# A four-layer graph network on one core: part of the second pass's product computed inside the first pass, from column tiles still on chip

## The reference, cut to what matters

```
x1 = LN(x  + adj @ (scale * (adj @ (x @ w0))) + bias0)       # layer 0: two products with adj
x2 = LN(x1 + relu(inv_deg * (a*adj + (1-a)*I) @ x1 @ W.T + b))   # layer 1: row sums of adj give inv_deg
x3 = LN(x2 + layer2(x2))    # one product for z, then distances z z^T, 4 nearest, second product
x4 = LN(x3 + relu([x3, adj @ x3] @ W.T + b))                 # layer 3
```

## Time and profile before

| what | us |
|---|---|
| runs: median of 3 | 1589.72 |
| runs: lowest, highest | 1587.08, 2805.07 |
| profiled execution, its own time | 1597.85 |
| profiled execution, span first to last instruction | 1596.3 |
| PE busy, PEld busy in that span | 1446.2, 748.6 |
| DVE, ACT, POOL busy | 836.0, 465.3, 208.9 |

### The profile page before, as it was taken

One profiled execution on the slowest core, in us unless ns is written; L12 is line 12 of the kernel. 1 busy time (PEld: TensorE's weight loads), 2 busy tenths in 40 slices (PEclk: granted clock), 3 DMA queues, 4 the chain that ended last, 5 costly groups with the idle time before them and its releaser, 6 DMA issues.

```text
span 1596.3 us, 20924 instructions
## 1 busy us (share of the span) xinstructions
PE 1446.2 (91%) x7300; PEld 748.6 (47%) x7300; DVE 836.0 (52%) x1278; ACT 465.3 (29%) x979; POOL 208.9 (13%) x267
## 2 busy tenths in 40 slices
PE   6888888887999999999999888999999499878997
PEld 4555555554444444444444433444444144433554
DVE  6667667664222133323222379999998046543122
ACT  4656565653000000000000056666665000000010
POOL 1111111110000000000000000000000447763000
PEclk9999999999999999999999999999999799989999
DMA  9999998888899888888777500013333889889773
GB/s 312 332 334 340 340 323 314 311 323 332 340 343 345 335 314 312 316 324 331 304 283 283 184 7 1 14 54 120 123 124 115 283 321 371 310 321 361 284 284 130
DMA packets 127677, 418.98 MB, mean 262 GB/s; under 512 B 10657, under 2 KB 44033, under 8 KB 104577
## 3 DMA queue, kind: packets, MB, share of 16 engines
q1 hardware_dynamic: 78272, 331.37, 55.9%
q0 software_dynamic: 19088, 71.83, 11.8%
q10 hardware_dynamic: 30256, 15.00, 3.2%
HBM read 353.14 MB, written 65.01 MB: 262 GB/s over the span
## 4 chain that ended last, share of the span: by engine, by line
PE 56%; DVE 16%; DMA 10%; issue 7%; POOL 5%; ACT 5%; DVEq 0%; ACTq 0%; POOLq 0%; SPq 0%
PE acc L1010 12%; PE acc L1011 12%; PE acc L1012 12%; POOL gath_all L434 5%; DVE hT L865 5%; DVE wz_sb L866 5%; DMA at_scratch<-region 4%; PE pt L1054 3%; DMA gath_all<-y_scratch,wz_sb 2%; DVE region L818 2%; PE pt L1116 2%; PE pt L1119 2%; PE pt L1118 2%; PE pt L1117 2%; PE pt L1012 2%
## 5 line engine op out<-in xcount | busy, mean ns | idle before, releaser
L1010 PE MATMUL acc<-region,yop 128*128 128x512 f16 x850 | 326.8, 385 | 63.7 <-DVE region L818 39.1
L1011 PE MATMUL acc<-region,yop 128*128 128x512 f16 x850 | 326.2, 384 | 0.0
L1012 PE MATMUL acc<-region,yop 128*128 128x512 f16 x850 | 325.8, 383 | 0.0
L592 ACT ACTIVATE region<-pt 128x512 f32<-128x512 f32 x256 | 149.8, 597 | 114.8 <-PE pt L1119 79.6
L818 DVE SCALAR_TENSOR_TENSOR region<-pt,region 128x512 f16<-128x512 f32 x200 | 128.9, 685 | 94.2 <-ACT region L499 93.5
L1054 PE MATMUL pt<-ident,region 128*128 128x128 f32 x1024 | 153.7, 278 | 8.3 <-DMA region<-in_adj 8.3
L1010 PEld LDWEIGHTS acc<-region,yop 128*128 128x128 f16 x850 | 83.6, 98 | 156.1 <-DVE region L818 51.2
L1054 PEld LDWEIGHTS pt<-ident,region 128*128 128x128 f32 x1024 | 129.7, 144 | 55.2 <-issue 9.5
L865 DVE MAX8 hT<-region 128x8 f32<-128x4096 f32 x32 | 141.5, 4421 | 11.4 <-ACT region L592 10.6
L499 ACT ACTIVATE region<-pt 128x512 f16<-128x512 f32 x200 | 112.6, 593 | 106.9 <-PE pt L1054 64.1
L1012 PEld LDWEIGHTS acc<-region,yop 128*128 128x128 f16 x850 | 83.9, 99 | 102.9 <-issue 4.4
(11 more groups left out here) (221 smaller groups left out, 1904.7 us busy)
## 6 DMA issues: line engine op xcount, KB each, us to landing
region<-at_scratch SPq DMA_DIRECT2D x180, 1280.0 KB, 7.3
region<-in_adj SPq DMA_DIRECT2D x64, 1024.0 KB, 9.0
at_scratch<-region POOLq DMA_DIRECT2D x40, 768.0 KB, 7.1
region<-at_scratch SPq DMA_DIRECT2D x100, 256.0 KB, 3.7
at_scratch<-region POOLq DMA_DIRECT2D x40, 512.0 KB, 7.5
x_scratch<-xout ACTq DMA_DIRECT2D x24, 256.0 KB, 6.2
yop<-in_x SPq DMA_DIRECT2D x4, 512.0 KB, 10.8
xin<-in_x POOLq DMA_DIRECT2D x8, 256.0 KB, 3.5
```

The lines of the kernel that those rows point to most:

```text
L592: nc.scalar.activation(near[i % 2][:, j * CHUNK:(j + 1) * CHUNK], pt[n % NEAR_BANKS][:, :], ACT.Copy).then_inc(near_copied, 1)
L1010: nc.tensor.matmul(into, y[:, 0, kt, :], high, start=(kt == 0), stop=False)
L1011: nc.tensor.matmul(into, y[:, 0, kt, :], low, start=False, stop=False)
L1012: return nc.tensor.matmul(into, y[:, 1, kt, :], high, start=False, stop=(kt == KT - 1))
```

## The change

1. **Early products.** `early_tiles(c)` = max(0, 4(c-1)): 0, 0, 4, 8, 12, 16, 20, 24 for the eight chunks. In pass 0, while chunk c's tile kt is on chip, PE also multiplies it by pass 1's operand tile kt, if kt is below `early_tiles(c)` (those operand tiles come from chunks up to c-2 of pass 0 and exist already). The sum goes into PSUM bank `pxT`. At kt = 30 of such a chunk ACT copies it, scaled, into `xT` and stores it to a new DRAM tensor `part_scratch`. In pass 1, chunk c begins at tile `early_tiles(c)`; POOL loads the stored part into `xT`, and DVE (in place of ACT) makes `hT` as acc + part, for c = 2 to 7.
2. **Loads of pass 1.** Only tiles that pass 1 still multiplies are loaded (`UNITS1`), the first unit of a chunk in part. The first chunk's five units wait each for its own stretch of the on-chip memory (`early_slot`) in place of one wait for all of pass 0.
3. **Row sums in pieces.** Each unit is summed in four 128x512 pieces, two on DVE (even kt) and two on ACT (odd kt).
4. **Lag.** `LAG` = 4, and it runs over chunk ends: the first four tiles of chunk c+1 are transposed between the products of chunk c's last four. Within a tile, transposes and products now alternate: transpose 0, (early products), product, transpose 1, product, transpose 2, product, transpose 3.
5. **Places.** Pass 0's `hT` copy on ACT at kt = 7 (was 8), PE's projection at kt = 11 (was 8), DVE's epilogue at kt = 14 and 15 (was 16). In pass 1 the projection is placed four tiles after the chunk's first tile. PE's code for passes 0 and 1 is written out for all eight chunks; ACT's for pass 0 for four of them.

The core of the diff:

```diff
-LAG = 3
+LAG = 4
+ROW_PIECES = 2
+    part_dram = nc.dram_tensor("part_scratch", [NCH, P, CHUNK], F32).ap()
+        def early_tiles(c):
+            return max(0, (c - 1) * TPC)
+
+        UNITS1 = [(c, u, max(0, early_tiles(c) - KEPT - u * UNIT)) for c in range(NCH) for u in range(UPC)
+                  if KEPT + (u + 1) * UNIT > early_tiles(c)]
...
@@ SP, load_natural @@
-                        half = c * (NAT_UNITS // 2) + (u - 4) // 2 + 1
-                        sp.wait_ge(rows_summed_dve if u % 2 == 0 else rows_summed_act, half)
+                        sp.wait_ge(rows_summed_dve, before * ROW_PIECES)
+                        sp.nop(nofuse=True)
+                        sp.wait_ge(rows_summed_act, before * ROW_PIECES)
...
-            sp.wait_ge(tr_done, NCH * KT)
-            sp.wait_ge(rows_summed_dve, NCH * NAT_UNITS // 2)
-            sp.wait_ge(rows_summed_act, NCH * NAT_UNITS // 2)
-            sp.wait_ge(acc_full, NCH)
-            for s in range(2):
-                for part in range(len(STORES)):
-                    sp.wait_ge(stage_stored[s][part], 16 * NCH * UPC // 2)
+            def early_slot(u):
+                done = (NCH - 1) * NAT_UNITS + min(6 + u, NAT_UNITS)
+                sp.wait_ge(tr_done, done * TPC)
+                sp.wait_ge(rows_summed_dve, done * ROW_PIECES)
+                sp.wait_ge(rows_summed_act, done * ROW_PIECES)
+                if u == UPC - 2:
+                    sp.wait_ge(stage_used, NCH * (UPC - 1))
+                if u == UPC - 1:
+                    sp.wait_ge(acc_full, NCH)
+                for s in range(2):
+                    units = NCH * UPC // 2 if u >= UPC - 2 + s else (UPC + 1 - s) // 2
+                    for part in range(len(STORES)):
+                        sp.wait_ge(stage_stored[s][part], 16 * units)
+
+            for k, (c, u, k0) in enumerate(UNITS1):
+                if c == 0:
+                    early_slot(u)
+                else:
+                    before = max(b for b in range(k) if UNITS1[b][1] == u)
+                    if u == UPC - 1:
+                        sp.wait_ge(acc_full, nth(ALL, 1, UNITS1[before][0]))
+                    else:
+                        sp.wait_ge(unit_used, used1(before))
+                sp.dma_start(ring[u][:, k0:, :, :].rearrange("p k h n -> p (k h n)"),
+                             at_dram[c, u, :, k0 * 2 * CHUNK:]).then_inc(unit_loaded[u], 16)
...
@@ POOL, pass 1 @@
+            for c in range(NCH):
+                if c == 2:
+                    pool.wait_ge(part_stored, 16 * (NCH - 2))
+                if c > 2:
+                    pool.wait_ge(hT_ready, nth(ALL, 1, c - 1))
+                if c >= 2:
+                    pool.dma_start(xT[:, :], part_dram[c, :, :]).then_inc(part_loaded, 16)
+                load_xin(1, x_dram[0], c, c == 0)
...
@@ ACT, split_high @@
-                    if kt % 8 == 6:
+                    if kt % 2 == 1:
+                        u, t = divmod(kt, TPC)
...
+                        nc.scalar.activation(discard[:, 0:CHUNK], nat[u % 4][:, t, :], ACT.Copy,
+                                             accum_out=rs_part[par][:, u, t:t + 1]).then_inc(rows_summed_act, 1)
...
+                    if kt == KT - 2 and not (isinstance(c, int) and c < 2):
+                        act.wait_ge(part_full, c - 1)
+                        if not isinstance(c, int) or c > 2:
+                            act.wait_ge(part_stored, 16 * (c - 2))
+                        nc.scalar.activation(xT[:, :], pxT[:, :], ACT.Copy, scale=1.0 / (A_SCALE * Y_SCALE[0])
+                                             ).then_inc(part_ready, 1)
+                        act.wait_ge(part_ready, c - 1)
+                        act.dma_start(part_dram[bass.ds(c, 1), :, :].rearrange("c p n -> (c p) n"), xT[:, :]
+                                      ).then_inc(part_stored, 16)
...
@@ DVE, epilogue of pass 1 @@
+                if p == 1 and not (isinstance(c, int) and c < 2):
+                    dve.wait_ge(part_loaded, 16 * (c - 1))
+                    dve.wait_ge(acc_full, n)
+                    dve.wait_ge(nat_full, n - 1)
+                    nc.vector.scalar_tensor_tensor(hT[:, :], acc[par][:, :], 1.0 / (A_SCALE * Y_SCALE[0]), xT[:, :],
+                                                   ALU.mult, ALU.add).then_inc(hT_ready, 1)
...
@@ DVE, split_low @@
-                    if kt % 8 == 2:
...
+                    if kt % 2 == 0:
+                        u, t = divmod(kt, TPC)
+                        if t == 0:
+                            dve.wait_ge(nat_loaded[u % 4], 16 * (c * 2 + u // 4 + 1))
+                        nc.vector.tensor_reduce(rs_part[par][:, u, t:t + 1], nat[u % 4][:, t, :],
+                                                AXX, ALU.add).then_inc(rows_summed_dve, 1)
...
@@ PE, pass 0 @@
+            def products_of(c, par, kt, between):
+                hi, lo = stored(c, par, kt)
+                pe.wait_ge(low_done, c * KT + kt + 1)
+                if kt < early_tiles(c):
...
+                    nc.tensor.matmul(pxT[:, :], yh, hi, start=(kt == 0), stop=False)
+                    nc.tensor.matmul(pxT[:, :], yh, lo, start=False, stop=False)
+                    early = nc.tensor.matmul(pxT[:, :], yl, hi, start=False, stop=final)
...
+                nc.tensor.matmul(acc[par][:, :], yh, hi, start=(kt == 0), stop=False)
+                between(1)
+                nc.tensor.matmul(acc[par][:, :], yh, lo, start=False, stop=False)
+                between(2)
+                last = nc.tensor.matmul(acc[par][:, :], yl, hi, start=False, stop=(kt == KT - 1))
...
+                    turn(0)
+                    if kt >= LAG:
+                        products_of(c, par, kt - LAG, turn)
+                    elif not first(c):
+                        products_of(c - 1, 1 - par, KT + kt - LAG, turn)
+                    else:
+                        turn(1)
+                        turn(2)
+                    turn(3)
...
@@ PE, pass 1 @@
+                        if p == 1 and kt < early_tiles(c):
+                            continue
```

More of the change, by code:

```diff
@@ L249, in late_loads, with each_chunk @@
             return LATE_SLOTS[:k].count(slot)
-        def each_chunk(eng, body):
-            body(0, 0, 0)
-            body(1, 1, 0)
-            with eng.Fori(1, NCH // 2) as pair:
+        def each_chunk(eng, body, unrolled=2):
+            for c in range(unrolled):
+                body(c, c % 2, c // 2)
+            with eng.Fori(unrolled // 2, NCH // 2) as pair:
                 body(pair * 2, 0, pair)
@@ new lines, in split_high @@
+                    if kt == 7 and not first(c):
+                        act_epilogue(act, 0, c - 1, 1 - par)
+                    if kt == KT - 2 and not (isinstance(c, int) and c < 2):
[7 more added lines that the diff above has]
+                                      ).then_inc(part_stored, 16)
@@ L837, in _ @@
             each_chunk(dve, split_low)
-            counted(0, NCH - 1, lambda: epilogue(0, NCH - 1, 1))
+            scale_projected(NCH - 1)
+            counted(0, NCH - 1, lambda: split_projected(NCH - 1))
             close(0)
@@ L1006, in pe_epilogue, with products @@
                 pe_epilogue_at(pe, kt, p, c)
-        def products(p, into, kt, high, low):
+        def products(p, into, kt, high, low, first_tile=0):
             y = yop[OPERAND[p]]
-            nc.tensor.matmul(into, y[:, 0, kt, :], high, start=(kt == 0), stop=False)
+            nc.tensor.matmul(into, y[:, 0, kt, :], high, start=(kt == first_tile), stop=False)
             nc.tensor.matmul(into, y[:, 0, kt, :], low, start=False, stop=False)
@@ L1027, in setup_transposes, with stored @@
                 nc.tensor.transpose(setup_rows, hT[0:rows_j, 0:P], ident[0:rows_j, 0:rows_j]).then_inc(setup_pe, 1)
-            def transposing_chunk(c, par, m):
-                def products_of(kt):
-                    pe.wait_ge(low_done, c * KT + kt + 1)
-                    if kt < KEPT:
-                        hi, lo = (kept[:, bass.ds(c, 1), kt, h, :].rearrange("p c n -> p (c n)") for h in range(2))
-                    else:
-                        s = (par * UPC + (kt - KEPT) // UNIT) % 2
-                        hi, lo = (stage[s][:, (kt - KEPT) % UNIT, h, :] for h in range(2))
-                    if first(c) and kt % XT_PART == 0:
-                        pe.wait_ge(y0_ready, kt // XT_PART + 1)
-                    if kt == 0 and not (isinstance(c, int) and c < 2):
-                        pe.wait_ge(hT_ready, c - 1)
-                    last = products(0, acc[par][:, :], kt, hi, lo)
-                    if kt == KT - 1:
-                        last.then_inc(acc_full, 1)
-                    elif kt >= KEPT and (kt - KEPT) % UNIT == UNIT - 1:
-                        last.then_inc(stage_used, 1)
+            def stored(c, par, kt):
+                if kt < KEPT:
+                    return [kept[:, bass.ds(c, 1), kt, h, :].rearrange("p c n -> p (c n)") for h in range(2)]
```

(10 more changed lines are left out.)

116 lines of the change are left out of this document (68 added, 48 removed).

## The result

The changed kernel takes 1549.01 us, median of 4 runs (1545.57 to 1577.11), against 1592.13 for the kernel before; the ratio is 0.970, 95% interval 0.966 to 0.975. The run of 1577.11 had a lower granted clock (0.931, the other three 0.974 to 0.978), and the kernel before has a run of 2805.07; the ratios leave such runs out. In a later set of runs, with five rounds, the same pair gave 1546.60 and 1594.44 us, ratio 0.969 (0.967 to 0.971). The profiled execution took 1545.57 us, span 1544.0, where the prediction had 1545 for it. The median forecast, 1537, was 12 us too low, well inside the range. That agreement hides two errors of opposite sign, and a wrong account of what earns the gain.

The account below looks back on a forecast made before the run. Pass 0 stalls in bursts above a 36 us PE and DMA floor; PE fills pass 1. The 555 us to pass 1's end become 377 + 125 = 502, 53 less: 1545 profiled, 1537 median, range 1508 to 1563.

Parts of the forecast that it names:

- The lag costs nothing: Pass 0 chunk ends: the lag adds no wait, and the end wait of some 2.5 us goes.
- Alternation is free: Pass 0 tiles: alternating transposes and products keeps the pitch at 1.085 us, bounds 1.05 and 1.25.
- D: Rival, pass 0: alternating exposes every weight load, 1.52 us per tile, 42 us slower, 1632 us; chance 0.04.
- The stop at the way into pass 1: Between passes 0 and 1: PE's 6.0 us stop and 3 us at half clock go, 9 us.
- the step "Pass 0 by chunks": Pass 0: chunk 0 55 us, chunks 1 to 3 42.5 each, 4 to 7 PE's need plus 1; sum 377.
- Rival A: Pass 0: smooth stores let chunks 1 to 3 take 38 us and not 42.5, -13 us, 1521 us; chance 0.13.
- the floor of 36: Pass 0: PE and DMA both need about 36 us per chunk; bursts keep them 9 us above it.
- the step "Pass 1": Pass 1: 125 us, chunks 0 to 5 101, chunks 6 and 7 10 each by late loads, 4 for traffic.
- 10.6 us per chunk at most: Pass 1's last chunks: the epilogue takes this long, about as long as a chunk limited by its load.
- Rival B: Pass 1 bound by its transfers at 347 GB/s: 9 to 15 us above 125, so 1546 to 1552; chance 0.15.
- wrong altogether if the stretch after pass 1 changed its length: Sign of failure: all the change touches lies in the first 555 us; the other 1040 stay.
- Rival C: Pass 0: stalls stay, from stores' landings, and moved products are paid in full: 1581 us; chance 0.10.

Follow-up runs that it names:

- e2: Changed kernel with row sums in whole units again on DVE and ACT: 1585.60 us, ratio 0.977 to the kernel before.
- e4: Changed kernel with each pass 0 chunk's last four products done before the next chunk's transposes (no lag over chunk ends): 1577.80 us, ratio 0.969 to the kernel before.
- f2: Changed kernel with no early products and no stored part, run again beside the changed kernel: 1538.50 us, ratio 0.964 to the kernel before.
- f1: The changed kernel itself, run again in a later set on another chip: 1546.60 us, ratio 0.969 to the kernel before.
- f4: Changed kernel with at most 4 early tiles per chunk (24 and not 84): 1531.96 us, ratio 0.961 to the kernel before.
- f3: Changed kernel without row sum pieces, lag over chunk ends (LAG = 3) and alternation; early products, slot loads, places stay: 1578.47 us, ratio 0.988 to the kernel before.
- e6: Changed kernel with pass 2's first residual load waiting for seven of pass 1's eight stores: 1539.74 us, ratio 0.962 to the kernel before.
- e7: Changed kernel with two buffers for pass 1's rows on their way out: 1548.19 us, ratio 0.967 to the kernel before.
- e8: Changed kernel with at most 16 early tiles per chunk, the earlier residual load and two output buffers together: 1535.82 us, ratio 0.961 to the kernel before.

## Why the prediction was right, and where it was wrong

**Right.** PE's idle time in pass 0 was there to be used, and the largest stall that an experiment shows were the row sum blocks (e2, 18 to 22 us). The lag costs nothing; what it gains is within the spread of two profiles (e4). Alternation is free: 1.09 us per tile against my 1.085, so D falls. The weight load of a transpose lies under the product ahead of it, and the rule of the Trainium skill ("TensorE: Matmul & The Clock Gate", Part 3, What overlaps and what doesn't) is not what full-height loads do here (by it a tile would take 1.52 us, my estimate in the prediction). The stop at the way into pass 1 went as worked out (6.0 to 0.38 us).

**Wrong: the step "Pass 0 by chunks", and with it the account of the gain.** I let chunks 1 to 3 take 42.5 us by the DMA and chunks 4 to 7 PE's need plus 1, sum 377, and said pass 0 "swallows 54 us of products". It ended at 364.6 and 368.4. Chunks 1 to 3 took 41.0, 39.2 and 42.4, chunks 4 to 6 took 43.4, 46.4 and 48.5, which is PE's bare need (43.7, 46.3, 48.9). Rival A, chunks 1 to 3 at 38 us and 13 us to gain, came true in part: with the early products they are 4.9 us better than my 127.5 (122.6 together), and at 38 us only without them (f2). The other 7.5 us lie in chunk 0 and in chunks 4 to 7; of the latter, 4 to 6 did without the 1 us each that I had added. Smoothed, pass 0 runs at 39 us a chunk without early products, 3 us above the floor of 36 that I had worked out myself from the earlier trace rows. I had the floor and did not draw the conclusion: when smoothing brings a chunk to 39 us, some 2 us of PE's time in each (12.4 in all, f2) are left to hide moved products in. The sum itself counts nothing twice, since each chunk pays PE's full need; what was wrong is to give the moved products the credit for idle time that the smoothing removes without them. I never worked out the time of the change without its first part.

**Wrong: the step "Pass 1".** I had 125; it took 133.2 and 137.8. The last chunks take 13.4, 13.1 and 15.4 us where I had 10.3 + 0.5, 10 and 10. The mechanism, a unit issued at the chunk's end that lands late, is the right one, and the loads that PE waited for in the last two chunks landed after 6.9, 9.1 and 5.7 us, near my 7.0 (the median over the pass is 8.7). What I left out stands behind the stops. The clock falls to about half behind the two longer ones (windows of 0.53 and 0.58), so that the five tiles behind them take 4.9 and 4.5 us and not 3.2. And I let the epilogue run beside the stop, "10.6 us per chunk at most"; in chunk 7 it runs behind it, since the turn comes after the tile that waits, and `hT` leaves 15.2 us after the one before. In f1 DVE waits 5.3 us more there for a store, and its last `hT` leaves 8.4 us after the products are done. Rival B forecast this length, by another cause: transfers at 347 GB/s. They moved 369 GB/s over the pass, and 419 in chunk 1, so that rate is not what bound it. The limit of about 358 GB/s that the Trainium skill states ("DMA: Bandwidth & Descriptors", Where 436 GB/s comes from) does not show either: this lone core moves 386 GB/s over pass 0 in f2 and 399 over pass 1 in f4.

**Missed: two waits.** Pass 1's rows leave through one buffer, and a store now needs 12.2 us to land in the median (6.2 before); DVE waits for it before the next chunk's rows (9.8 us in all), and PE pays behind it, at the last `hT` of pass 1 (5.7 us in f1) or at the residual load of pass 2 behind the last store (6.51 us in the first profile). I had asked what is late next for the loads, and not for the stores. The prediction would be "wrong altogether if the stretch after pass 1 changed its length": it did in the first profile, from 1041.4 to 1046.2 us, by this wait (f1 has 1040.7).

**The sum.** Pass 0 12 us better than forecast, pass 1 8 us worse, the stretch after it 5 worse (pass 2 6 us longer): 52 us in place of 53 for the profiled execution. The number was right by compensation, which is luck. The change without the moved products gives 56 us by itself; all 84 tiles of them, in which the prediction saw the gain, cost 8 of these, while 24 tiles (f4) add 6.5.

Rival C ("every moved product is paid in full") had a price for them near the one measured (43.8 of 54.2 us) and the wrong reason: not because stalls remain, but because they had gone. Where the stalls remain (f3) the products cost less, 24.7 us, with what the places gain in it.

**Not tried:** the places of `hT`'s copy and projection, whose wait before was 12.6 us, by themselves; the PE code written out; ACT's pieces without DVE's; the loads by slot alone; why e6's and f4's timed runs are faster than their marks; early tiles between 4 and 16 per chunk.

## What to carry to other kernels

Before moving work into an engine's idle time, work out how long the stage takes once its stalls are gone: if that is near the engine's own need, removing the stalls and filling them are the same gain, and only one can be had. Test the parts of such a change one by one; here the parts around the main one (shorter blocks on helper engines, other places for the epilogue, a lag over the loop's end, loads that wait only for their own slot) earned more than the whole. When a stage gets shorter per chunk, every fixed latency in it (load, store, residual) comes up against the shortest chunk, so move only as much as keeps the shortest chunk longer than the slowest landing, and see whether the epilogue then runs beside that landing or behind it. When an edit removes a wait and the time stays, look for the same late event at the next place that waits for it (e6, e7, e8).

## What the runs showed of the hardware

Landing times are longer where the DMA's share is higher. Ring loads of 1.25 MiB in pass 1 took 6.9 us in the median before (share 0.90), 7.4 in f2 (0.91), 8.8 in f1 (0.95), 8.9 in f4 and 9.1 in e8 (1.00). Stores of 256 KB in pass 1 took 6.2 us before and in f2, 12.2 in the changed kernel, 17.4 in f4 and 17.0 in e8. PE hardly waits for the slow stores of f4 and e8 (1.4 and 0.2 us at the residual load): f4's late chunks take 18.5 us, about as long as its slowest store (18.7), and e8 has two buffers. With loads and stores mixed, one core moved 386 GB/s over all of pass 0 (f2) at a share of 1.02, where the kernel before moved 321. The nearly unchanged code behind the third mark took 859 to 896 us by set and execution, more than most of these edits are worth: compare within one set of runs, and by marks.
